# Node windows halved to 16, basis parts read in permuted column order, and the turned inputs split from PSUM on VectorE

## The reference, cut to what matters

```python
xw  = x @ W0.T                                   # 625 x 512
h   = D^-1/2 (A + I) D^-1/2 xw ; batch norm, gelu, + x, + x, layer norm
w_r = einsum('rb,bio->rio', att, basis)          # 30 bases of 512x512 for each of 2 layers: 64 MB in the kernel's reads
msg = where(edge_type == 0, gate_0 * x_j @ w_0, gate_1 * x_j @ w_1)
out = segment_sum(msg, row) + x @ root + bias    # layer 1 with relu, then layer 2; residual, layer norm
```

## Time and profile before

| | |
|---|---|
| median of 3 runs (lowest to highest) | 328.7 us (328.42 to 328.86) |
| the profiled execution | 328.01 us, of which the span of the trace is 326.2 us |
| busy in the span: PE, DVE, ACT, POOL | 291.7, 179.9, 140.9, 48.1 us |
| first `oh_key` instruction, last add into B, first AT instruction | 16.69, 96.59, 98.06 us |
| basis parts read by SP | 64 of 1024 KB |

### The profile page before, as it was taken

The page is one execution under the profiler, slowest core; times in us unless marked ns, Lnnn a source line. Parts: engine busy times, 40 slices in busy tenths (PEclk is TensorE's granted clock), DMA queues, the critical chain, the costliest instruction groups (busy, mean ns, idle before and its releaser), DMA issues.

```text
span 326.2 us, 4834 instructions
## 1 busy us (share of the span) xinstructions
PE 291.7 (89%) x1709; PEld 198.1 (61%) x1709; DVE 179.9 (55%) x502; ACT 140.9 (43%) x274; POOL 48.1 (15%) x80
## 2 busy tenths in 40 slices
PE   0778999997898999647999999999997999999991
PEld 0644656643336668414686655657796877787771
DVE  3789987999979755688401024035246125433333
ACT  5499997989710458748225213220412242100000
POOL 2334400000000920372000000000001900010000
PEclk9999999999796799969999999999999999999997
DMA  6972888599797799909999578979000510001112
GB/s 174 341 318 96 332 330 291 245 395 420 293 393 304 257 317 409 401 36 335 418 353 406 194 280 337 378 280 363 13 0 0 132 31 0 2 0 32 31 33 63
DMA packets 12757, 73.66 MB, mean 226 GB/s; under 512 B 1952, under 2 KB 2195, under 8 KB 4540
## 3 DMA queue, kind: packets, MB, share of 16 engines
q1 hardware_dynamic: 11282, 70.82, 57.1%
q0 software_dynamic: 1104, 2.36, 2.9%
q10 hardware_dynamic: 346, 0.17, 0.2%
HBM read 72.05 MB, written 1.28 MB: 225 GB/s over the span
## 4 chain that ended last, share of the span: by engine, by line
PE 69%; DVE 16%; DMA 5%; issue 5%; ACT 1%; POOL 1%; DVEq 1%; SPq 0%; POOLq 0%
PE psW L490 13%; PE psM L471 11%; PE psM L473 10%; PE psM L472 10%; PE psM L712 7%; PE psM L732 6%; PE psE L566 5%; DVE oh_key L1050 4%; PE psM L618 3%; DMA basis_ring<-in_L_gnn_basis_dram 3%; DMA xs<-in_x_dram 3%; DVE w L1033 1%; DVE B L1040 1%; DVE x_sum L1167 1%; DVE AT L1100 1%
## 5 line engine op out<-in xcount | busy, mean ns | idle before, releaser
L490 PE MATMUL psW<-basis_ring,S 128*32 128x512 f32 x512 | 65.9, 634 | 1.0 <-DMA basis_ring<-in_L_gnn_basis_dram 1.0
L1050 DVE TENSOR_SCALAR oh_key<-iota_f,key 128x320 f16<-128x320 f16 x162 | 46.8, 330 | 4.9 <-DVE B L1040 1.7
L1214 DVE SCALAR_TENSOR_TENSOR zg<-psM,gate,zg 125x512 fp32r<-125x512 f32 x20 | 15.0, 751 | 57.9 <-ACT zg L904 57.9
L566 PE MATMUL psE<-oh_key,oh_src 128*125 128x320 f16 x162 | 35.6, 340 | 5.5 <-DVEq L1042 3.7
L566 PEld LDWEIGHTS psE<-oh_key,oh_src 128*125 128x125 f16 x162 | 21.9, 145 | 25.2 <-issue 13.9
L780 ACT ACTIVATE oh_diff<-iota_f,edgeT 128x128 f16<-128x128 f16 x108 | 34.3, 389 | 1.5 <-ACT xT_full L794 0.8
L904 ACT ACTIVATE zg<-psM,gate 125x512 fp32r<-125x512 f32 x20 | 13.8, 689 | 46.1 <-PE psM L473 45.7
L471 PE MATMUL psM<-w,hlT 128*125 128x512 f32 x80 | 32.4, 405 | 0.1
L490 PEld LDWEIGHTS psW<-basis_ring,S 128*32 128x32 f32 x512 | 13.7, 113 | 29.8 <-issue 26.1
L473 PE MATMUL psM<-w,hlT 128*125 128x512 f32 x80 | 31.6, 395 | 0.0
L472 PE MATMUL psM<-w,hlT 128*125 128x512 f32 x80 | 31.6, 395 | 0.0
(11 more groups left out here) (161 smaller groups left out, 451.3 us busy)
## 6 DMA issues: line engine op xcount, KB each, us to landing
basis_ring<-in_L_gnn_basis_dram SPq DMA_DIRECT2D x64, 1024.0 KB, 6.8
root_raw<-in_L_gnn_root_dram POOLq DMA_DIRECT2D x32, 64.0 KB, 3.5
xs<-in_x_dram SPq DMA_DIRECT2D x1, 1120.0 KB
out_dram<-xs SPq DMA_DIRECT2D x5, 224.0 KB
w_raw<-in_L_gnn_W_dram SPq DMA_DIRECT2D x1, 1024.0 KB, 10.4
bias_b<-in_L_gnn_bias_dram POOLq DMA_DIRECT2D x1, 250.0 KB, 3.3
xs<-in_x_dram SPq DMA_DIRECT2D x1, 130.0 KB
out_dram<-xs SPq DMA_DIRECT2D x5, 26.0 KB
```

What stands on the lines that cost most here:

```text
L490: m = nc.tensor.matmul(psW[32 * j:32 * j + 32, cc % 2, :], S[:, cc % 2, cc // CH, q].rearrange("p k r -> p (k r)"), ring[:, n % RING, j, : ...
L566: nc.tensor.matmul(psE[0:PC, g % 2, 0:KEYS], oh_src[:, g % 3, j * P:j * P + PC], oh_key[:, t % OH, :], start=(j == 0), stop=(j == G - 1)). ...
L1050: v.tensor_scalar(oh_key[:, t % OH, :], iota_f[:, 0:KEYS], key[:, t:t + 1], None, ALU.is_equal) \
L1214: link(v.scalar_tensor_tensor(out=zg[:, 1, c, r, :], in0=bank(("Z", L, c, r))[0:PC, :], scalar=gate[:, L, c, r:r + 1], in1=zg[:, 0, c, r, ...
```

## The change

Windows become 16 nodes wide and belong to 3 tiles (SG): NW = 54 windows, KEYS = 160, and each half of `psE` holds the two windows of a group side by side. DVE adds two windows a group, at tiles 1 and 3 of the group after next, and no longer waits for an add right behind it; the next add waits for it. On the data of the reference the destinations of 3 tiles differ by at most 13, so the loop over further rounds still isn't entered.

ACT now makes only the high part of a turned block, DVE subtracts it from the bank (`turned_low`, reading PSUM), and POOL does none of it. The PE turns are spread otherwise over the first groups, and the base matmul comes ahead of them. `build_S` moves one group earlier, `rounds` to group 12. The first 32 basis parts stream `natural(ring[...])`, with a step of 16 elements (64 bytes), so that `psW`, `half` and `both` have the wanted order, and `w_high` and `w_low` read and write without a step.

```diff
@@ -50,14 +50,16 @@
-W = 32
+SG = 3
+NW = T // SG
+W = 16
@@ -242,13 +244,11 @@
+        use("base", "dve")
         turned = [("xT", 0), ("xT", 1)] + [("w0T", k) for k in range(KC)] + [("xT", c) for c in range(2, NC)]
-        for name in turned[0:2]:
-            use(name, "act")
-        use("base", "dve")
         use("att", "dve")
-        for name in turned[2:]:
-            use(name, "act")
+        for name in turned:
+            use(name, "dve")
...
-        FIRST_TURNS = 4
+        FIRST_TURNS = 3
+        TURN_AT = {0: (3,), 1: (4, 5), 2: (6, 7), 3: (8,)}
+        TURNED_LOW_AT = {1: (0, 1), 2: (2, 3), 3: (4, 5), 4: (6, 7), 5: (8,)}
+        ROUNDS_AT = 12
...
-            for i, (what, c) in enumerate(turned):
-                pool.wait_ge(in_hi, i + 1)
...
-                nc.gpsimd.tensor_tensor(lo, full, hi.bitcast(F32), ALU.subtract).then_inc(in_lo, 1)
...
-                                         ring[:, n % RING, j, :], start=(q == 0), stop=(q == SUB - 1))
+                                         natural(ring[:, n % RING, j, :]) if cc < CH else ring[:, n % RING, j, :],
+                                         start=(q == 0), stop=(q == SUB - 1))
...
-            for i in range(2):
-                turn(i)
             pe.wait_ge(base_ready, 1)
...
                 if g >= 2:
-                    pe.wait_ge(win_added, g - 1)
+                    pe.wait_ge(win_added, 2 * (g - 1))
...
-                    nc.tensor.matmul(psE[0:PC, g % 2, 0:KEYS], oh_src[:, g % 3, j * P:j * P + PC],
-                                     oh_key[:, t % OH, :], start=(j == 0), stop=(j == G - 1)).then_inc(adj_used, 1)
-                if g + FIRST_TURNS < len(turned):
-                    turn(g + FIRST_TURNS)
+                    at = j // SG * KEYS
+                    nc.tensor.matmul(psE[0:PC, g % 2, at:at + KEYS], oh_src[:, g % 3, j * P:j * P + PC],
+                                     oh_key[:, t % OH, :], start=(j % SG == 0), stop=(j % SG == SG - 1)) \
+                        .then_inc(adj_used, 1)
+                for i in TURN_AT.get(g, ()):
+                    turn(i)
...
-                    if pp < KC:
-                        hi, full = in_q(hi), natural(full)
                     nc.scalar.activation(hi, full, ACT.Copy).then_inc(w_hi, 1)
...
+            def turned_high(i):
+                wait_full(act, turned[i])
+                hi, _, ps = turned_parts(i)
+                nc.scalar.activation(hi, ps, ACT.Copy).then_inc(in_hi, 1)
...
+            def turned_low(i):
+
+                dve.wait_ge(in_hi, i + 1)
+                hi, lo, ps = turned_parts(i)
+                link(v.tensor_tensor(lo, ps, hi.bitcast(F32), ALU.subtract))
+                dve.sem_inc(free_dve, 1)
+                dve.sem_inc(in_lo, 1)
...
-                    if pp < KC:
-                        lo, full, hi = in_q(lo), natural(full), in_q(hi)
                     v.tensor_tensor(lo, full, hi, ALU.subtract).then_inc(w_lo, 1)
...
+                if h == 0:
+                    dve.wait_ge(adj_used, G * (g + 1))
+                if w:
+                    dve.wait_ge(win_added, w)
                 to = B[:, :, :, bass.ds(at, W)]
-                link(v.tensor_tensor(to, to, psE[0:PC, g % 2, 0:NC * WIN].rearrange("p (c t w) -> p c t w", c=NC, t=R),
-                                     ALU.add))
-                dve.sem_inc(win_added, 1)
+                v.tensor_tensor(to, to, psE[0:PC, g % 2, h * KEYS:(h + 1) * KEYS]
+                                .rearrange("p (c t w) -> p c t w", c=NC, t=R), ALU.add).then_inc(win_added, 1)
...
-            add_window(NG - 2)
-            add_window(NG - 1)
+            for w in range(NW - 4, NW):
+                add_window(w)
+            dve.wait_ge(win_added, NW)
```

More of the change, by code:

```diff
@@ L59 @@
 V_GATE, V_BIAS1, V_B, V_GAMMA, V_BETA, NV = 0, 2 * R, 2 * R + 1, 2 * R + 2, 2 * R + 3, 2 * R + 4
-assert T == NG * G and T == 2 * ROWS and G % 2 == 0
+assert T == NG * G and T == 2 * ROWS and G == 2 * SG
 KB = 16
@@ L157, in gnn_block @@
         ones_f = sb("ones_f", [P, P], F32)
-        mm = sb("mm", [ROWS, 2], F32)
-        gmm = sb("gmm", [1, 4, NG], F32)
-        base_i = sb("base_i", [1, NG], I32)
+        mm = sb("mm", [ROWS, 2, 2], F32)
+        gmm = sb("gmm", [1, 4, NW], F32)
+        base_i = sb("base_i", [1, NW], I32)
         spans = sb("spans", [1, MAXW], F32)
@@ L335, in own, with turned_parts @@
             return BG * q - bases(q).start
+        def turned_parts(i):
+            what, c = turned[i]
+            n = slice(c * PC, (c + 1) * PC)
+            if what == "xT":
+                return xT_hi[:, :, n], xT_lo[:, :, n], bank(turned[i])[:, 0:KC * PC].rearrange("p (k n) -> p k n", k=KC)
+            return w0T_hi[:, c, :], w0T_lo[:, c, :], bank(turned[i])
         def w_block(L, kc):
@@ L512, in _ @@
             pe.wait_ge(minmax_ready, 1)
-            for i in range(2):
-                last[0] = nc.tensor.transpose(bank("minmax")[0:1, i * ROWS:(i + 1) * ROWS], mm[:, i:i + 1],
+            for i, h in itertools.product(range(2), range(2)):
+                last[0] = nc.tensor.transpose(bank("minmax")[0:1, i * T + h:(i + 1) * T:2], mm[:, i, h:h + 1],
                                               ident[0:ROWS, 0:ROWS])
@@ L541, in xw_part @@
                     done()
-            for i in range(2):
-                turn(i)
             pe.wait_ge(base_ready, 1)
             wait_free(pe, "base")
-            last[0] = nc.tensor.matmul(bank("base")[:, 0:NG], ones_f[0:1, :], gmm[0:1, 0, :], start=True, stop=True)
+            last[0] = nc.tensor.matmul(bank("base")[:, 0:NW], ones_f[0:1, :], gmm[0:1, 0, :], start=True, stop=True)
             done()
@@ L556, in _ @@
             done()
-            for i in range(2, FIRST_TURNS):
+            for i in range(FIRST_TURNS):
                 turn(i)
@@ L787, in places @@
                                      bias=ones_f[:, 0:1], scale=-1.0).then_inc(src_ready, 1)
-            def parts(full, hi, ps, name):
-                wait_full(act, name)
-                nc.scalar.activation(hi, ps, ACT.Copy).then_inc(achain, 1)
-                chained[0] += 1
-                ins = nc.scalar.activation(full, ps, ACT.Copy)
-                ins.then_inc(achain, 1)
-                chained[0] += 1
-                act.wait_ge(achain, chained[0])
-                act.sem_inc(free_act, 1)
-                act.sem_inc(in_hi, 1)
             act.wait_ge(consts, 4)
@@ L826, in _ @@
                     release(nc.scalar.activation(xw[:, c, :], bank(("xw", c))[0:PC, :], ACT.Copy), ("xw", c), "act")
-                if g + 2 < len(turned):
-                    turned_parts(g + 2)
+                for i in TURNED_LOW_AT.get(g, ()):
+                    turned_high(i)
             w_first(2)
@@ L1051, in _ @@
                     .then_inc(key_ready, 1)
-                if t == 2 * G - 1:
+                if t == G - 1:
+                    v.tensor_copy(base_i[:], gmm[0:1, 0, :])
                     build_S()
+                    dve.wait_ge(b_zero, 1)
+                if t % G == G - 1:
+                    for i in TURNED_LOW_AT.get(t // G, ()):
+                        turned_low(i)
+                if t == ROUNDS_AT * G:
                     rounds()
-                    dve.wait_ge(b_zero, 1)
-                if t % G == 1 and t > 2 * G:
-                    add_window(t // G - 2)
+                if t % G in (1, 3) and t > 2 * G:
+                    add_window(t // SG - 4)
                 if t % G == 3 and t // G in MERGE_AT:
```

40 lines of the change are left out of this document (13 added, 27 removed).

## The result

The changed kernel takes 339.86 us (median of 4 runs, 339.72 to 339.99) where the kernel before takes 328.78 (328.42 to 330.5): a ratio of 1.033 (95% interval 1.030 to 1.035), slower. The forecast was 316.8 us and faster. The profiled execution after took 339.99 us, its span is 338.2.

A forecast was written before the change was run, and what follows sets the result against it. The edge stage before AT was taken as bounded in turn by DVE, PE and DMA transfers, the transfers deciding after the change. 328.0 - 11.4 - 0.5 = 316.1, with the median 0.7 above: 316.8 us, range 310 to 327.

The forecast's parts named there:

- The step in the ring's rows ... nothing: PE's first 32 basis parts: 0.92 ns an element at the step is what parts already take, so no cost.
- a part is 1.78 us: PE's stepped basis parts: the step halves the rate of the parts themselves; the slower rival, chance 0.16.
- The rival's own sum: Stepped parts cost twice: AT at 95.3, 6.1 us more behind the stage, 331.5 us in all, slower; chance 0.16.
- What hides the second register load: DVE's adds in the edge stage: the sequencer runs ahead, two loads fit a 1.82 us group with nothing to spare.
- no shorter DVE group: Edge stage rival: exposed loads or PE's half clock keep groups at 2.2 to 2.3 us, 326 us in all; chance 0.13.
- the charge for the clock: End of the edge stage: 1.0 us charged for PE's clock; AT's gain of 12.4 us becomes 11.4.
- the 0.24 us for an add of 160 elements: DVE's two adds in a steady group: each counted at 0.24 us within 1.82 us a group.
- 2.9: DMA latency of parts issued from 64.23 us on: about 2.9 us beside 10.4 us of transfer.
- the way from `rows_f` to the first key: Ahead of the edge stage: waits and POOL stalls go, 2.6 us saved, first key at 14.1 us.
- The transfers as a wait of PE: Late edge stage: part 21 lands at 81.0, PE's last tile product at 82.9, so transfers decide over DVE's 80.9.
- Nothing behind the stage but 0.5 us: After AT: the trace only shifts, with 0.5 us saved by block 2's splits at 127 us.

The follow-up runs named there:

- e1_plain: Changed kernel with the ring read in plain order again and the first 32 parts' splits stepped as before, windows of 16 kept: 326.54 us, 0.992 of the kernel before.
- e9_w16_fixed: Changed kernel with plain ring, windows of 16 and add addresses fixed in code instead of loaded (output not the reference's): 320.3 us, 0.973 of the kernel before.
- e7_pairs: Changed kernel with windows of 32, one add a group, earlier register loads, first 32 parts read in pairs of neighbours: 322.36 us, 0.981 of the kernel before.

## Why the prediction was wrong, by its own steps

**The failed step: "The step in the ring's rows ... nothing".** The working took ACT's row, in which the step nearly doubles the time (1.04 us for 0.57), turned it into 0.92 ns an element "at PE's fastest rate", and found the parts as slow as that already. A least time for an element read at that step was the right kind of price, but its size was off by a factor of two: the parts showed 1.8 ns, against the 0.9 that a plain part takes, and `xw`'s products 0.84 to 0.9 against 0.45. So the term that the sum had at nothing measured 1.9 us a pair, 13 us in all. The prediction had this outcome in the same paragraph ("a part is 1.78 us"; measured 1.85 to 1.95) and gave it 0.16. ACT's own row had been nearly a doubling of the engine's time; the argument that the parts ran slowly anyway compared them with a rate of `xw`, and no row gave the price of a step for either.

**The rival's own sum**, 331.5, was 8 us short. Behind the stage it came out, though not by its own terms (5.2 for three pairs and 0.9 for the pair behind the degrees, less 0.5 for the splits, is 5.6; measured 5.7, and the three pairs alone make that). The pair behind the degrees ran at the half clock before, at 3.64 us, and so cost 0.15 more and not 1.9. In the stage it put AT at 95.3, measured 104.4: group 4 started 2.4 us later than in that sum, groups 4 to 13 took 38.7 for 37.5, and groups 14 to 26 28.7 for 23.9. PE and DVE took turns to wait: DVE waited 5.6 us for `psE` in groups 4 to 13 and 2.6 behind them, and PE then 1.15 and 0.96 for adds, since DVE's merges, splits and adds were no longer hidden. That this accounts for the whole 4.8 isn't shown.

**"What hides the second register load"** failed too, and would have spoiled the forecast alone: with the ring plain the time is 326.5, not 316.8. The two rows were read in a steady group, where the sequencer does run ahead (e1_plain's group is 1.81 to 1.84 us, as predicted). In the groups with low parts, merges and splits, and among the last adds, it doesn't. It measured 6.3 us; the rival "no shorter DVE group" had the right time (326) by luck, with the load in the steady groups, where it cost nothing.

**What is left**, 320.3 for 316.8: the edge rows landed 1.0 us later than in the profile of before, which is within what they move by anyway; the two splits still have their step there (1.4 on DVE); and in its stage of DVE and parts in turn a pair took 3.35 us and half a pair 1.93, behind waits of PE, where the charge for the clock was 1.0. These add up to more than the 3.5 us, so part of them is covered.

**Two terms of the sum.** No run shows the 1.0 us that the sum charges for the clock, the author's estimate; in its place, that pair and half pair of e9_w16_fixed (at 83.95 and 73.54 us) took 3.35 and 1.93 us for 1.92 and 1.06 elsewhere, 2.3 us more, with a granted clock of 0.83 from 75 to 90 us. No row of before shows the 0.24 us for an add of 160 elements, an estimate too; the runs showed 0.32 us with a pitch of 0.24, as it had it.

**Two readings that were off**, with little weight: the granted clock in the earlier trace rows is below full in the slices from 98 to 114 us, and not to 106 only; and 13.5 less 10.4 us is 3.1 us of latency where the sum went on with 2.9.

**Right:** the way from `rows_f` to the first key, 7.5 us instead of 10.0 (2.5 for a forecast 2.6); keys at a pitch of 0.17, adds at 0.32 with a pitch of 0.24, the nine stalls beside POOL gone but for one key of 1.04 us; products at 0.07 to 0.09 us. The transfers as a wait of PE: in e1_plain a part lands at 79.34 after 2.1 us of waiting, with a step of 9.18 us in the chain; but DVE's list, the longer by the loads, still had 17 us to go from there. "Nothing behind the stage but 0.5 us" held in e7_pairs within what can be told.

## What to carry to other kernels

Before the order of a matmul's moving operand is changed, count how many neighbouring elements it takes at a time. Here, at the full clock, plain fp32 parts kept their rate with two (2.00 us a pair for 1.92) and fp32r products with four (a pitch of 0.24 us for 0.23), and with single elements at steps of 4 and 16 both took about twice as long (3.8 us and 0.43 to 0.46), however much slower the one kind was than the other. If another engine needs the permuted order, give it the last step: pairs on PE cost nothing here (a mean MATMUL of 634 ns with and without), and a step of 8 bytes next to nothing (645 against 620 ns on ACT, 688 against 686 on DVE). An add whose address comes from a loaded register cost the sequencer about half a microsecond here (in e1_plain 303 ns for the load, 183, 23 and 52 for the address), hidden in the group of the earlier trace rows and in the open, for 0.43 us, where 0.34 us of keys was all that was queued ahead of it: look at the places behind a wait, not at the steady loop.

## What the runs showed of the hardware

- With a single one of the four strips stepped a pair took 3.61 us against 1.92 for a plain one; with all four 3.8 to 4.1.
- A stepped pair takes 3.79 us at a granted clock of 0.58 and of 1.00 alike; a plain one takes 1.85 at 1.00 and 3.64 at 0.50. The step cost 1.9 us at 1.00 and 0.15 or less at 0.50 to 0.58.
- A step of 3 elements cost three quarters of what steps of 4, 8 and 16 cost (2.89 us a pair against 3.8). A step of 64 cost more than one of 16 (4.25 and 4.62 us against 3.87), which nothing here explains.
- fp32r products had a pitch of 0.24 us with runs of four elements (0.23 plain), with runs of two 0.43, with single elements 0.43 to 0.46. That two neighbours cost them as much as single ones no run here explains.
- The DMAs of the edge rows, the first issued at 1.2 us in each, let `rows_f` start anywhere from 6.45 to 8.30 us; about 1 us of such chance lies in every comparison of single profiles above.
